# A fused transformer megakernel: in the first cross attention, value projections move beside the first score halves

## What is computed

```
def _L0_xattn_ref(q, k, v, wq, bq, wk, bk, wv, bv, wo, bo):      # NH = 16 heads of D = 16
    qh = (q @ wq + bq).reshape(b, -1, NH, D).transpose(0, 2, 1, 3)
    kh = (k @ wk + bk).reshape(b, -1, NH, D).transpose(0, 2, 1, 3)
    vh = (v @ wv + bv).reshape(b, -1, NH, D).transpose(0, 2, 1, 3)
    attn = jnp.einsum('bhqd,bhkd->bhqk', qh, kh) / SCALE
    score = jax.nn.softmax(attn, axis=-1)
    out = jnp.einsum('bhqk,bhkd->bhqd', score, vh)
    ...
x = x + _L0_xattn_ref(_layernorm(x, axis=-1), ctx_1024, ctx_1024, ...)
```

## Time and profile before

| what | us |
|---|---|
| median of three executions | 2355.11 (2352.07 to 2359.96) |
| the profiled execution, its own time | 2351.33 |
| its span, first to last instruction | 2349.1 |
| TensorE busy (matmuls) | 2168.8 (92%) |
| VectorE, ScalarE, GpSimd busy | 1315.5, 997.3, 331.6 |
| mean granted TensorE clock | 0.959 |

### The profile page before, as it was taken

One profiled execution on the slowest core, in us unless ns is written; L12 is line 12 of the kernel. 1 busy time (PEld: TensorE's weight loads), 2 busy tenths in 40 slices (PEclk: granted clock), 3 DMA queues, 4 the chain that ended last, 5 costly groups with the idle time before them and its releaser, 6 DMA issues. The chain is left out here.

```text
span 2349.1 us, 39843 instructions
## 1 busy us (share of the span) xinstructions
PE 2168.8 (92%) x15922; PEld 1499.2 (64%) x15922; DVE 1315.5 (56%) x2292; ACT 997.3 (42%) x1868; POOL 331.6 (14%) x366
## 2 busy tenths in 40 slices
PE   7999999999999977999998899978999999887796
PEld 4777777777777754555554677854555554545795
DVE  4566666656665634555553344447777772667554
ACT  1555555555555552333433011114666665516121
POOL 3322222232222200000000000014000000000241
PEclk9999999999999978999999899998999999898798
DMA  6877776777777521000000212113111111013312
GB/s 200 197 171 183 179 174 154 173 178 171 183 178 176 127 59 51 6 12 6 6 1 1 115 68 94 55 45 78 28 33 36 24 24 31 23 43 136 135 48 78
DMA packets 101338, 216.18 MB, mean 92 GB/s; under 512 B 58738, under 2 KB 66299, under 8 KB 95428
## 3 DMA queue, kind: packets, MB, share of 16 engines
q1 hardware_dynamic: 98420, 204.93, 35.3%
q0 software_dynamic: 2208, 6.03, 0.8%
q10 hardware_dynamic: 528, 2.69, 0.4%
HBM read 91.16 MB, written 15.20 MB: 45 GB/s over the span
## 5 line engine op out<-in xcount | busy, mean ns | idle before, releaser
L1089 DVE TENSOR_REDUCE L_xattn_maxima<-L_xattn_scores 128x1 f32<-128x1024 f32 (+1 forms) x256 | 253.6, 991 | 239.4 <-PE L_xattn_scores L1012 239.0
L1156 ACT ACTIVATE L_xattn_probs_t<-L_xattn_turned 128x1024 f32<-128x1024 f32 (+1 forms) x256 | 220.8, 862 | 332.6 <-PE L_xattn_turned L1024 332.6
L1997 DVE TENSOR_REDUCE shared_half_maxima<-shared_ring 128x1 f32<-128x578 f32 (+1 forms) x251 | 244.4, 991 | 89.9 <-PE shared_ring L1903 87.1
L2077 ACT ACTIVATE shared_exps<-shared_scores 128x512 f32<-128x512 f32 (+1 forms) x416 | 225.7, 594 | 122.6 <-PE shared_scores L1924 122.0
L1168 ACT ACTIVATE L_xattn_probs<-L_xattn_scores,L_xattn_maxima 128x1024 f32<-128x1024 f32 (+1 forms) x256 | 235.6, 925 | 37.7 <-DVE L_xattn_maxima L1092 37.7
L1024 PEld LDWEIGHTS L_xattn_turned<-ident,L_xattn_probs 128*128 128x128 f32 x1664 | 197.3, 144 | 79.7 <-issue 46.7
L1024 PE MATMUL L_xattn_turned<-ident,L_xattn_probs 128*128 128x128 f32 x1664 | 233.9, 280 | 12.9 <-ACT L_xattn_probs_t L1156 12.0
L686 PE MATMUL L_xattn_projected<-L_xattn_wv,L_xattn_ctx 128*128 128x256 f32 x780 | 193.0, 389 | 0.0
L680 PE MATMUL L_xattn_projected<-L_xattn_ctx,L_xattn_wk 128*128 128x400 f32 x480 | 182.0, 501 | 0.0
L1012 PE MATMUL L_xattn_scores<-L_xattn_k_stack,L_xattn_q_stack 128*128 128x512 f32 (+1 forms) x512 | 159.0, 392 | 22.2 <-ACT L_xattn_probs L1168 11.0
L1924 PE MATMUL shared_scores<-shared_q,shared_k 128*128 128x512 f32 (+1 forms) x416 | 154.1, 449 | 0.1
(11 more groups left out here) (392 smaller groups left out, 3152.7 us busy)
## 6 DMA issues: line engine op xcount, KB each, us to landing
L_xattn_k_stack<-L_xattn_k_part SPq DMA_DIRECT2D x504, 200.2 KB, 4.3
L_xattn_ctx<-in_ctx_t SPq DMA_DIRECT2D x16, 1602.0 KB, 7.0
ffn_task<-in_ffn_task SPq DMA_DIRECT2D x16, 1024.0 KB, 6.7
experts_w_in<-in_expert_in SPq DMA_DIRECT2D x8, 1024.0 KB, 11.5
shared_k<-k_scratch SPq DMA_DIRECT2D x64, 100.1 KB, 3.3
L_xattn_q_stack<-q_scratch SPq DMA_DIRECT2D x128, 32.0 KB, 2.0
k_scratch<-L_xattn_shared_part SPq DMA_DIRECT2D x128, 32.0 KB, 1.7
shared_q<-q_scratch SPq DMA_DIRECT2D x64, 64.0 KB, 3.6
```

What stands on the lines that cost most here:

```text
L1089: nc.vector.reduce_max(maxima[n % 2][:, half:half + 1], cols, axis=AX).then_inc(halves_maxed, 1)
L1156: nc.scalar.activation(probs_t[:, t:t + m, p * P:(p + 1) * P], turned_tiles[:, 0:m, :], ACT.Copy).then_inc(turned_moved, 1)
L1997: nc.vector.reduce_max(half_maxima[:, n, half:half + 1], found[:, 0:HALF_STARTS[half + 1] - HALF_STARTS[half]], axis=AX).then_inc(ring_max ...
L2077: nc.scalar.activation(exps[n % 2][0:m, h * BANK:(h + 1) * BANK], scores[0:m, h, :], ACT.Exp, scale=SCALE).then_inc(exps_done, 1)
```

## The change

Every batch now projects five of its seven values units (2 to 6) in its own steps 0 to 4, beside the first score halves. The shared unit and values units 0 and 1 of the batch after stand beside the first halves of steps 5 to 7, and the eight keys units of the batch after beside the second halves. The turn unit stays last. `slots` lists this, as pairs of (batches ahead, unit); `order_of` gives each unit its place in the counts of the two projection semaphores. Batch 15 now has its five own values units.

In `first_block` values units 2 to 6 of batch 0 are gone. The context of batch 0 comes in four transfers of 400 columns; keys 0 is projected ahead of the transposes of x, keys 1 between their two halves, keys 2 between the second and third query product, the rest behind the queries. ScalarE's queue takes half of `load_q` of batch 0.

SyncE's queue loads the context of the batch two ahead after pair 3, into the buffer that the batch's own values used, and stores the shared part after pair 7.

```
-    odd_units = [("shared", 0)] + [("values", i) for i in range(V_UNITS)]
-    units = [unit for i in range(K_UNITS) for unit in (("keys", i), odd_units[i])] + [("turn", 0)]
+    first_units = [("keys", i) for i in range(K_UNITS)] + [("shared", 0), ("values", 0), ("values", 1), ("turn", 0)]
+    odd_slots = [(0, ("values", i)) for i in range(2, V_UNITS)] + [(1, ("shared", 0)), (1, ("values", 0)), (1, ("values", 1))]
+    slots = [slot for i in range(K_UNITS) for slot in (odd_slots[i], (1, ("keys", i)))] + [(1, ("turn", 0))]
+    def order_of(b, unit):
+        if b == 0 and unit in first_units:
+            return first_units.index(unit)
+        if (0, unit) in slots:
+            return FIRST_UNITS + U * b + (slots if b < BATCH - 1 else last_slots).index((0, unit))
+        return FIRST_UNITS + U * (b - 1) + slots.index((1, unit))
...
+                def fill(b, i, last):
+                    ahead, unit = slots[i]
+                    if ahead == 0 or not last:
+                        project(pe, b + ahead, unit, projected[:, 0], order_of(b + ahead, unit))
+
                 def batch(b, parity, first, last):
                     for n in range(PAIRS):
                         score(b, parity, n, 0)
-                        if not last:
-                            project(pe, b + 1, 1 - parity, 2 * n, projected[:, 0], U * (b + 1) + 2 * n)
+                        fill(b, 2 * n, last)
...
                         score(b, parity, n, 1)
-                        if not last:
-                            project(pe, b + 1, 1 - parity, 2 * n + 1, projected[:, 0], U * (b + 1) + 2 * n + 1)
+                        fill(b, 2 * n + 1, last)
...
                         stack_keys(sp, n)
-                        if n == GROUP_PAIRS - 1:
-                            store_shared(sp, b + 1)
+                        if n == GROUP_PAIRS - 1 and ctx_left:
+                            sp.wait_ge(projection_done, order_of(b, ("values", V_UNITS - 1)) + 1)
+                            load_ctx(sp, b + 2, parity)
+                    store_shared(sp, b + 1)
                     if q_left:
                         load_q(sp, b + 2, parity)
-                    if ctx_left:
-                        sp.wait_ge(projection_done, U * (b + 2))
-                        load_ctx(sp, b + 3, 1 - parity)
...
+                    pe.wait_ge(keys_loaded, 32)
+                    pe.wait_ge(bank_ready, 1)
+                    project_first(0)
                     pe.wait_ge(ident_loaded, 16)
                     for t in range(TILES):
...
+                        if t == TILES // 2 - 1:
+                            project_first(1)
...
-                    load_q(sp, 0, 0)
+                    load_q(sp, 0, 0, range(0, COPIES // 2))
...
+                    act.wait_ge(zeros_ready, 4)
+                    act.wait_ge(query_stored, 16 * 2 * len(q_units))
+                    load_q(act, 0, 0, range(COPIES // 2, COPIES))
```

More of the change, by code:

```diff
@@ L616, in load_ctx, with load_q @@
             sp.dma_start(ctx[parity][:], dram["ctx_t"][ds(b, 1)].rearrange("o p c n -> (o p) c n")).then_inc(ctx_loaded[parity], 16)
-        def load_q(sp, b, parity):
-            for copy in range(COPIES):
+        def load_q(sp, b, parity, copies=range(COPIES)):
+            for copy in copies:
                 for e in range(2):
@@ L654, in split_shared @@
         def split_shared(pool, b):
[L655 removed]
+            pool.wait_ge(projection_moved, order_of(b, ("shared", 0)) + 1)
             if b > 0:
@@ L663, in split_parts @@
         def split_parts(pool, b):
-            for what, i in units:
+            for what, i in first_units if b == 0 else [unit for ahead, unit in slots if ahead == 1]:
                 if what == "keys":
@@ L668, in split_parts, with project @@
                     split_shared(pool, b)
-        def project(pe, b, parity, u, bank, moved):
-            if u == 0:
-                pe.wait_ge(ctx_loaded[parity], 8 * (b - parity) + 16)
+        def project(pe, b, unit, bank, moved):
+            parity = b % 2
+            what, n = unit
+            if what == "keys" and n == 0 and b > 0:
+                pe.wait_ge(ctx_loaded[parity], 8 * (b + parity))
             if moved > 0:
                 pe.wait_ge(projection_moved, moved)
-            what, n = units[u]
             if what == "keys":
@@ L700, in project, with move_projection @@
             last.then_inc(projection_done, 1)
-        def move_projection(dve, b, parity, u, bank):
-            dve.wait_ge(projection_done, U * b + u + 1)
-            what, n = units[u]
+        def move_projection(dve, b, unit, bank):
+            parity = b % 2
+            what, n = unit
+            dve.wait_ge(projection_done, order_of(b, unit) + 1)
             if what == "keys":
@@ L752, in first_block @@
             keys_loaded = core.sem(first, f"{layer}_keys_loaded")
+            columns_loaded = [core.sem(first, f"{layer}_columns_loaded{i}") for i in range(CHUNKS_PER_GROUP)]
+            shared_loaded = core.sem(first, f"{layer}_shared_loaded")
             values_loaded = core.sem(first, f"{layer}_values_loaded")
@@ L812, in _, with project_first @@
                 def _(pe):
+                    def project_first(u):
+                        what, n = first_units[u]
+                        if what == "keys" and n < CHUNKS_PER_GROUP:
+                            pe.wait_ge(columns_loaded[n], 16)
+                        if what == "shared":
+                            pe.wait_ge(shared_loaded, 32)
+                        if what == "values":
+                            pe.wait_ge(values_loaded, 16)
+                        project(pe, 0, first_units[u], banks[:, u % 4], max(u - 3, 0) if what != "turn" else u)
+                    pe.wait_ge(keys_loaded, 32)
+                    pe.wait_ge(bank_ready, 1)
+                    project_first(0)
                     pe.wait_ge(ident_loaded, 16)
@@ L821, in _ @@
                             last.then_inc(x_turned_ready, 1)
[L823 to L832, removed]
+                        if t == TILES // 2 - 1:
+                            project_first(1)
                     pe.wait_ge(query_loaded, 32)
                     for i, (m, half) in enumerate(q_units):
+                        if i == CHUNKS:
+                            project_first(2)
                         pe.wait_ge(x_turned_moved, half + 1)
@@ L1070, in batch @@
                             turn(b - 1, PAIRS - 1, 1)
-                        if n == PAIRS - 1 and not last:
-                            project(pe, b + 1, 1 - parity, U - 1, projected[:, 0], U * (b + 1) + U - 1)
+                        if n == PAIRS - 1:
+                            fill(b, U - 1, last)
                 pe.wait_ge(bank_zeroed, 1)
@@ L1119, in keep_heads, with move_slot @@
                                             ALU.add).then_inc(heads_ready, 1)
+                def move_slot(b, i, last):
+                    ahead, unit = slots[i]
+                    if ahead == 0 or not last:
+                        move_projection(dve, b + ahead, unit, projected[:, 0])
                 def batch(b, parity, first, last):
```

57 lines of the change are left out of this document (30 added, 27 removed).

## The result

The changed kernel takes 2388.7 us (median of six executions, 2382.45 to 2394.57) against 2357.7 for the kernel before in the same comparison: a ratio of 1.0133, 95% interval 1.0107 to 1.016.

A forecast was written before the change was run, and what follows sets the result against it. The prediction took a 2.94 us chain over three engines, plus h0, to bound each step of the first attention. 2351.3 + 48 (steady batches) - 8.5 (opening) + 0 (batch 15) = 2391, median 2395 us; range 2376 to 2407.

The forecast's parts named there:

- A step is h0 plus 2.94: In the first attention, a step lasts h0 (0.54, first unit, 0.79) plus a 2.94 us chain covering half 1's unit.
- Rival (a): TensorE bounds the steps and the 0.3 us before a score is its own: 2346 us, faster; chance 8%.
- Steady batches, +48: Batches 0 to 14: 2.8 us a batch beside half 0 plus 0.4 at its end, fifteen times: +48 us.
- The end of a batch: Turn unit behind keys unit 7 instead of the half-size unit: +0.4 us a batch, bounds 0 and 0.8.
- Opening, -8.5: Opening block: the queues decide its end, and its barrier comes earlier by 8.5 us, between -10.2 and -7.6.
- nearer the transfers: Opening's queues: between -10.2 and -7.6 us, taken closer to the case where transfers, not issues, took the time.
- The bound of -10.2: Opening: if each queue keeps its 8.26 us, the barrier comes at 41 instead of 51.44 us.
- The context's load: Context load in each batch, issued at 43.5 us, lands at 51, first read at 58: cover 7 us, cost nothing.
- rival (b): The context comes late: its load lands at 60, 2 us late, 14 times: +28, 2423 us; chance 5%.
- Batch 15, 0: Batch 15 gains five units beside half 0: taken as 0 us, bounds -2 and +8.
- rival (c): Granted clock falls to 0.50 in steady batches: steps over 9 us, the stage some 400 us more; chance 1%.
- The sum: On the profiled execution 2351.3 + 48 - 8.5 + 0 = 2391 us; median 3.8 above it, so 2395.

The follow-up runs named there:

- experiments 1 to 3: Half of each values unit left out in the kernel before (2355.9 us) and in the changed kernel (2313.5 us); units exchanged in the kernel before (2383.3 us).
- half_unit_last: Changed kernel with keys units beside half 0, own-batch values units 0 to 4, half-size unit ahead of the turn unit: 2346.6 us, again 2342.7 us.
- experiment 6: New opening alone with all seven values units and old step order, ratio 0.9971; then changed kernel with one queue for the queries of batch 0, 2387.2 us.
- experiment 7, values_first_in_batch_0: half_unit_last with the values unit beside half 0 and the keys unit beside half 1 in steps 0 and 1 of batch 0 alone: 2339.4 us.
- before: The kernel before, without the change: 2357.7 us beside the changed kernel.
- swap_before: Kernel before with only the exchange: in steps 2 to 7 the values unit beside half 0, the keys unit beside half 1: 2383.3 us, ratio 1.0117.
- half_values_before: Kernel before with half of each values unit left out in batches 1 to 15: 2355.9 us.
- opening_only: Kernel before with the new opening alone, all seven values units of batch 0 still in it, old order in the steps: ratio 0.9971.
- changed_again: The changed kernel once more, without any edit: 2383.6 us, ratio 1.0134.
- one_queue_after: Changed kernel with all eight loads of the queries of batch 0 on SyncE's queue: 2387.2 us.
- keys_first_after: Changed kernel with the two units of every step exchanged, keys beside half 0, new opening, own-batch values and context load kept: 2362.6 us, ratio 1.0031.

## Why the prediction was right, point by point

**A step is h0 plus 2.94: right.** The distance after half 1 kept its value under a keys unit, a values unit, half a values unit and nothing. Rival (a) forecast 2346; experiments 1 to 3 exclude it. The row that spoke for it, "issue" 98 times, was the wait for ScalarE's exponential all along: that row still says "issue" (96 times), but with a wait twice as long the products behind the weight load stand idle too, and there ScalarE is named. The prediction's reading of the two rows as 98 + 15 waits, one in each step, was wrong: 14 of the 15 are the batch starts, which are among the 98, and the step behind the shared unit has none. The waits were in seven steps of eight.

**Steady batches, +48: measured +39.9.** The mis-sized term is the unit beside half 0. I priced a values unit at 1.81 from its place behind half 1; beside half 0 it takes 1.73 (440.08 to 441.81). In turn a keys unit takes 1.43 beside half 1 (442.95 to 444.38) where it took 1.35. So the same products cost 0.08 more beside half 1 than beside half 0. They follow a score product of 66 columns there and one of 512 here; that this is the reason is argued and not shown. The half-size unit's step is 0.49 shorter than a keys step, the shared unit's 0.38 longer (I had 0.50). Together 2.2 us a batch instead of 2.8. The end of a batch cost 0.15 + 0.33 = 0.48 instead of 0.4, and its instants came as worked out: turn 2.68 and score 3.09 after half 1 (2.68 and 3.08 forecast). The 3.62 that the prediction gives for the old first unit is a slip: it started at 3.48 (2.94 + 0.54), and 0.4 is the difference to that.

**Opening, -8.5: measured -13.5.** Two steps failed. The queries were ready at 27.4, not 29.5: with keys unit 0 at work from 8.88, keys unit 1 between the transposes took 1.43 us (13.02 to 14.45) and not the 2.87 of the old first unit, the transposes behind it 0.90 and not 1.73, and the query products followed at 15.35. Why the old unit was slow isn't shown: "the low clock" was inferred from its length, while the profile has a granted clock of 1.00 both there (15.2 to 18) and in the changed kernel's stretch, and in `half_unit_last` the same unit at the same place takes 1.81. And I lay "nearer the transfers" where the issues decided: half of `load_q` took 1.8 and not 3.0, with the other queue not yet stacking beside it, and each queue kept 8.46 for its stacks with the other one busy. The rule of the Trainium skill (Trainium Kernel Development and Optimization, Key Constraints), that a second issuing engine saves only sequencer time, is borne out by the 4.9 us of experiment 6: issue time was what the path held. My conclusion from it, that the gain would be the smaller one, was what failed. The transfers' bill came one step later, as the landing at 48.3 of experiment 7; that the changed order covers it is luck, nothing in the forecast asked for it. The bound of -10.2 has a slip too: 29.5 + 3.0 + 8.26 is 40.8, which gives -10.7. The mean gain of about 12 lies beyond either.

**The context's load: right.** SyncE's queue in batch 8 of the changed kernel (which starts at 472.06), and the loads' times to landing over batches 1 to 14:

```profile
515.65 0.97 SPq L629 DMA_DIRECT2D L_xattn_ctx<-in_ctx_t  x1
...
DMA to landing us min/median/max: 7.7/8.5/9.1
```

It is issued 43.6 us into the batch (43.5 forecast) and landed at 524.1, 5.8 us ahead of its first reader at 529.9. Nothing waited for it, so rival (b) didn't come about, but the load took 8.5 us where it took 7.0: the cover was 7 on paper and under 6 in fact.

**Batch 15, 0: measured +2.1,** for reasons that the rows tell only in part. From the start of batch 15 to the output projection the granted clock falls to 0.50 at different points, and the length goes with the time spent there:

| kernels | units in batch 15 | us | of them at 0.50 |
|---|---|---|---|
| `before`, `swap_before`, `half_values_before` | none | 67.1, 67.2, 65.7 | 41.0, 44.4, 37.5 |
| `opening_only` | none | 62.6 | 23.9 |
| changed kernel, `changed_again`, `one_queue_after` | beside half 0 | 69.2, 69.0, 69.1 | 27.3 in each |
| `half_unit_last` and again | beside half 1 | 61.4, 61.5 | 20.5 in each |
| `keys_first_after`, `values_first_in_batch_0` | beside half 1 | 59.6, 60.2 | 13.7 in each |

With the very same work there `opening_only` is 4.5 us shorter than the kernel before, at 17 us less of the low clock. So both halves of the forecast's term came about: the five units beside half 0 cost time, and more of the stage ran at the full clock. As an estimate, on a line through `opening_only` and `before` a stage without units and with 27.3 us at 0.50 would take 63.5, so the units cost 5.6 and the clock gave back 3.6. That the net is near the forecast's 0 is luck. What makes the clock fall at one point or another stays open. In the steady batches the clock stayed at 1.00 throughout: rival (c) didn't come about.

**The sum.** It came 8 us too high in the batches and 5 us too high in the opening; both errors point the same way, 13 us in all. On the profiled execution the forecast was 8 too high only because batch 15 (+2.1) and the rest of the program (+3.0), which were forecast at nothing, took up 5 by luck. The range has a slip: its own terms added end to end give 2381 to 2414, not 2406. The result lies inside either.

## What to carry to other kernels

A busy share of 92% doesn't say that the order of work is free: find the wait that ends last in one repetition, split the repetition at it, and put movable work on the side that another engine's chain already covers. Before two units change places, read the distances on both sides of that wait; a unit moved out of cover is paid in full, one moved into it saves nothing. What a faster start brings forward, here a second issuing queue, shows up as the landing time of its transfers in the next block, so ask there what had cover before.

## What the runs showed that I had not expected

TensorE stops for 1 to 2 us at single places in the first attention with nothing that the trace could name. Two examples from TensorE's timeline, of `half_unit_last` and of `keys_first_after`:

```profile
651.27 0.31 PE L1067 MATMUL L_xattn_weighed<-L_xattn_probs_t,L_xattn_v 65*32 65x128 f32 x3 [1.71 <-issue]
```

```profile
663.59 0.31 PE L1067 MATMUL L_xattn_weighed<-L_xattn_probs_t,L_xattn_v 65*32 65x128 f32 x3 [1.73 <-issue]
```

They belong largely to the program: both profiles of the changed kernel have their longest batches at the same two places (batch 3, 54.87 and 54.87; batch 11, 54.28 and 54.31), and `half_unit_last` and its repetition both at batch 4 (53.67 and 52.88). The first of the two also had 55.02 in batch 11, the second not. A variant that shifts instructions thus gains or loses some us that have nothing to do with its idea; `keys_first_after` lost about 8 this way. What TensorE waits for there stays open.

The rest of the program, the same instructions in all kernels, took from 1456.5 us (`swap_before`) to 1472.9 (`values_first_in_batch_0`) between the start of the output projection and the end of the span. It goes with the clock: TensorE's granted clock was 0.50 for 149 us of the first and 193 of the second. So much of the scatter between single totals comes from there and not from the change, and the distances within a step decide more than a single time.
